# An attention stage on one core: the weighing of values done two key blocks at a time, value products and output projections moved to other slots

## The reference

```
c_q = h @ w_down_q.T ; c_kv = h @ w_down_kv.T              # latents, 128 wide
q, k, v = (c_q @ w_up_q.T), (c_kv @ w_up_k.T), (c_kv @ w_up_v.T)   # 16 heads of 64
q = _apply_rope_subspace(q, DR) ; k = _apply_rope_subspace(k, DR)
scores = jnp.einsum('bhqd,bhkd->bhqk', q, k) * scale
attn = jax.nn.softmax(scores, axis=-1)
out = jnp.einsum('bhqk,bhkd->bhqd', attn, v)
out = out.transpose(0, 2, 1, 3).reshape(b, s, H * DH)
out = out @ w_out.T + residual
```

## Time and profile before

| | |
|---|---|
| time, median of 3 runs | 2236.87 us (2235.29 to 2241.66) |
| the profiled execution's own time | 2242.25 us |
| its span, first to last instruction | 2240.6 us |
| mean granted TensorE clock | 0.940 |
| TensorE busy | 1922.1 us, 86% |
| VectorE, GpSimd busy | 1301.0 us, 1328.1 us |
| ScalarE busy | 895.0 us |
| instructions | 35323 |

### The profile page before, as it was taken

The page is one execution under the profiler, slowest core; times in us unless marked ns, Lnnn a source line. Parts: engine busy times, 40 slices in busy tenths (PEclk is TensorE's granted clock), DMA queues, the critical chain, the costliest instruction groups (busy, mean ns, idle before and its releaser), DMA issues. The chain is left out here.

```text
span 2240.6 us, 35323 instructions
## 1 busy us (share of the span) xinstructions
PE 1922.1 (86%) x12804; PEld 1333.1 (59%) x12804; DVE 1301.0 (58%) x1857; ACT 895.0 (40%) x1536; POOL 1328.1 (59%) x860
## 2 busy tenths in 40 slices
PE   5777649999999999999999964888885699998798
PEld 4666524454454545454454533666764699998798
DVE  6666436666656565666656523676663466565343
ACT  4554324433434343433434212333321355554454
POOL 2333228886868687887878632544544566666533
PEclk9888869999999999999999977999997899999899
DMA  3212231323222231323232213122213433323122
GB/s 102 75 56 75 86 106 40 76 48 95 57 67 69 50 93 34 95 48 95 57 85 58 57 29 126 32 70 77 61 57 105 133 81 81 77 51 107 29 45 42
DMA packets 81606, 158.63 MB, mean 71 GB/s; under 512 B 14496, under 2 KB 63520, under 8 KB 75552
## 3 DMA queue, kind: packets, MB, share of 16 engines
q1 hardware_dynamic: 66464, 133.40, 21.2%
q0 software_dynamic: 14592, 18.40, 5.0%
q10 hardware_dynamic: 432, 5.24, 0.6%
HBM read 80.84 MB, written 44.17 MB: 56 GB/s over the span
## 5 line engine op out<-in xcount | busy, mean ns | idle before, releaser
L916 ACT ACTIVATE a_pr<-a_pT 128x1024 f32<-128x1024 f32 x256 | 262.1, 1024 | 432.4 <-PE a_pT L739 432.4
L949 POOL TENSOR_TENSOR a_total<-a_total,a_pr 128x1024 f32<-128x1024 f32 x128 | 321.0, 2507 | 149.9 <-ACT a_pr L916 149.5
L821 DVE TENSOR_REDUCE a_row_max<-a_pG 128x2 f32<-128x1024 f32 x256 | 309.2, 1220 | 148.7 <-PE a_pG L713 148.6
L1832 DVE TENSOR_TENSOR c_h_lo<-c_h,c_h_hi 128x256 fp32r<-128x256 f32 x288 | 213.0, 757 | 195.0 <-ACT c_h_hi L1811 176.9
L752 PE MATMUL a_pA<-a_pr,a_v 128*64 128x512 f32 x1024 | 277.0, 619 | 0.1
L1811 ACT ACTIVATE c_h<-c_pU,c_b_c 128x256 f32<-128x256 f32 x288 | 138.8, 482 | 235.1 <-PE c_pU L103 234.5
L949 POOL TENSOR_TENSOR a_total<-a_pr 128x1024 f32<-128x1024 f32 x64 | 151.7, 2370 | 59.7 <-ACT a_pr L916 59.5
L930 POOL TENSOR_TENSOR a_by_cos<-a_by_cos,a_swapped 128x1024 f32<-128x1024 f32 x64 | 155.1, 2424 | 46.3 <-DMA a_swapped<-a_by_sin 46.2
L815 DVE TENSOR_TENSOR a_by_sin<-a_pG,a_sin 128x1024 f32<-128x1024 f32 x64 | 78.4, 1225 | 141.9 <-PE a_pG L103 136.9
L937 POOL TENSOR_TENSOR a_qk_lo<-a_by_cos,a_qk_hi 128x1024 fp32r<-128x1024 f32 x64 | 158.9, 2483 | 2.3 <-ACT a_qk_hi L886 2.3
L1868 POOL DMA_INDIRECT out_x<-c_y,c_ids x72 | 114.7, 1593 | 41.4 <-DVE c_y L1840 22.7
(11 more groups left out here) (248 smaller groups left out, 5072.7 us busy)
## 6 DMA issues: line engine op xcount, KB each, us to landing
a_swapped<-a_by_sin SPq DMA_DIRECT2D x256, 128.0 KB, 2.3
a_inv_by_head<-mid_inverses SPq DMA_DIRECT2D x32, 512.0 KB, 6.0
c_x_t<-mid_rows SPq DMA_DIRECT2D x37, 272.0 KB, 2.8
mid_latents<-f_c_parts SPq DMA_DIRECT2D x8, 1024.0 KB, 3.9
a_latent_parts<-mid_latents SPq DMA_DIRECT2D x8, 1024.0 KB, 7.2
d_raw<-in_weights SPq DMA_DIRECT2D x3, 2048.0 KB, 8.4
c_raw<-in_weights SPq DMA_DIRECT2D x3, 2048.0 KB, 8.1
f_x_t<-in_x SPq DMA_DIRECT2D x8, 512.0 KB, 3.9
```

The lines of the kernel that those rows point to most:

```text
L821: nc.vector.reduce_max(row_max[:, u % 2, :, t], pair[:], AX.X).then_inc(read, 1)
L916: nc.scalar.activation(pr[:, n % RP, :, :], pT[:], ACT.Exp, scale=SCALE).then_inc(exp_done, 1)
L949: nc.gpsimd.tensor_tensor(total[:, u % 2, :, :], before, pr[:, n % RP, :, :], ALU.add).then_inc(summed, 1)
L1832: nc.vector.tensor_tensor(h_lo[:, m % RH, :], h[:, m % RH, :], h_hi[:, m % RH, :], ALU.subtract).then_inc(h_lo_done[m % RH], 1)
```

## The change

In the order of TensorE's queue, `weigh` is called for two blocks of keys directly after each other: behind `shifted(u, 0)` the blocks 2 and 3 of the unit before, behind `shifted(u, 2)` the blocks 0 and 1 of the same unit. Behind `shifted` of slots 1 and 3 there is no weighing; in slot 1 `collect_sums` remains. Value products and output projections move from slots 1 and 2 to slots 1 and 3, in all queues at once. In slot 3 they stand behind `shifted` and ahead of `transpose_maxima`; on VectorE the addition stands ahead of `negate`, on ScalarE the copies ahead of the cast. After the last unit two weighings are left instead of one. Every instruction stays as it was; only the order changes.

```
@@ out_at and values_at
-            return (b - 1, 2 * (p - 3) + t - 1) if b >= 1 and p in (3, 4) and t in (1, 2) else None
+            return (b - 1, 2 * (p - 3) + t // 2) if b >= 1 and p in (3, 4) and t in (1, 3) else None
...
-            if p == 1 and t in (1, 2):
-                return b, 1, t - 1
-            if p == NP - 1 and t in (1, 2) and b + 1 < B:
-                return b + 1, 0, t - 1
+            if p == 1 and t in (1, 3):
+                return b, 1, t // 2
+            if p == NP - 1 and t in (1, 3) and b + 1 < B:
+                return b + 1, 0, t // 2
@@ TensorE's queue
                         shifted(u, t)
-                        if t >= 1:
-                            weigh(u, t - 1)
-                        elif u >= 1:
-                            weigh(u - 1, NT - 1)
+                        if t == 2:
+                            weigh(u, 0)
+                            weigh(u, 1)
+                        elif t == 0 and u >= 1:
+                            weigh(u - 1, 2)
+                            weigh(u - 1, 3)
...
-                weigh(UNITS - 1, NT - 1)
+                weigh(UNITS - 1, 2)
+                weigh(UNITS - 1, 3)
```

## The result

The changed kernel takes 2274.9 us (median of 4 runs, 2271.6 to 2280.7), the kernel before 2236.1 in the same comparison: ratio 1.018, 95% interval 1.016 to 1.020. The profiled execution of the changed kernel took 2276.02 us, 33.8 more than that of before.

The account below looks back on a forecast made before the run. TensorE's in-order queue, work and waits together, was taken as the bound. Unit terms sum to 5.98 us per batch element, 48 for eight, less 1 for the last unit: +47, 2284 us against the median 2236.87, range 2268 to 2303.

Parts of the forecast that it names:

- A second weighing costs 0.86, C alone 1.01: TensorE step prices in us: a weighing pair 1.87 instead of 1.01; C, collecting of sums, without a weighing 1.01.
- Plain unit +1.02: p = 0, 2, 5: +0.86 slot 0, -0.86 and +0.16 slot 1, +0.86 slot 2, nothing saved slot 3; +1.02 us.
- N: TensorE's transposing of the maxima, in slot 3; in plain units it waits for VectorE and cannot start before M2 + 3.04.
- M2: TensorE's scores for the row maximum, slot 2 (M0 to M3 for slots 0 to 3); VectorE takes the maximum.
- M1: Maximum scores of slot 1; needs the buffer Q filled, so waits for the second rotation product, ending at Q + 4.05.
- Unit with V +0.64: p = 1, 7, V being value products: +0.86 slot 0, 0 slot 1, -0.22 slots 2 and 3 together; sum +0.64 us.
- Q: TensorE's queries and keys matmuls, 1.59 us; the added weighing in slot 0 stands ahead of them.
- Unit with O +0.90: p = 3, 4, O being output projection (3.65 us): +0.86 - 0.22, and +0.26 from the later negation; sum +0.90 us.
- p = 5 and p = 6 +0.86: Both units together: latents load moves by only 0.86, its wait takes up 1.02, then -0.86 and +0.86; sum +0.86 us.
- first rival: The clock: new 1.45 us waits in plain units lower TensorE's clock, up to 36 us more, 2302 to 2320; chance 0.08.
- second rival: Faster: TensorE's own work decides, fewer tiling changes give -18 us, 2219; chance 0.05.
- third rival: No change: GpSimd sets the unit's length and TensorE's order doesn't matter, 2237 us; chance 0.04.

Follow-up runs that it names:

- experiment 3: Both orders with the maximum over 128 of 512 scores: changed order 2.8 us longer in attention; exponential also cut to 128 of 512 queries: 11.1 shorter.
- joined version: Kernel before with value products and output projections in slots 1 and 3, slot 2's maximum scores early, slot 0's weighing moved into slot 1: 2269.1 us, ratio 1.0115.
- experiments 1, 2 and 3: 1: kernel before with weighing pairs alone, 1.028, or products moved alone, 0.9966; 2: changed kernel, slot 2's maximum scores ahead of its pair, 1.0064; 3: see experiment 3.

## Why the prediction was right

The forecast was 2284 and +47, measured 2275 and +39 (33.6 in the traces). The mechanism came out as forecast: a weighing taken out of slots 1 and 3 lays bare waits for VectorE, and the second weighing in slots 0 and 2 is paid in full. The range of 2268 to 2303 held, but with 7 us to spare and a term that was off by 11. Term by term, in the element shown:

- *A second weighing costs 0.86, C alone 1.01.* Right: a pair 1.86, C with its wait 1.15.
- *Plain unit +1.02.* Right: p = 2 +1.03, by the three steps named (N held at M2 + 3.04, M1 held by the rotation product, two times 0.86 without cover). For p = 0 it was +0.65 (13.10 to 13.75): I took it as plain, but VectorE's reciprocal already made N wait longer in it.
- *Unit with V +0.64.* Right: p = 1 15.91 to 16.52, +0.61. V of slot 1 stands at the same distance from Q, 5.2.
- *Unit with O +0.90.* The 0.26 of the negation falls into the next unit: p = 3, 4 and 5 rose by 0.57, 0.80 and 1.27, together 2.64, forecast 0.90 + 0.90 + 1.02 = 2.82.
- *p = 5 and p = 6 +0.86.* The term that was mis-sized: 12.72 + 14.83 = 27.55 became 27.75, +0.20, of which 0.26 belong to O. Over all eight, p = 5 and 6 together changed by -2.5 us (from the first matmuls of the units), where 6.9 and 1.8 for O were forecast: 11 of the 13 us by which the sum was too large against the traces; p = 0 is most of the rest. What TensorE waited for in the 64 units before (in total, times, longest):

```profile
PE a_pG L720 <- DVE a_row_max L821: 15.6, 34, 0.7
PE a_pG L101 <- DMA a_latent_parts<-mid_latents: 10.4, 7, 2.6
PE a_pG L713 <- ACT a_qk_hi L886: 3.9, 4, 3.0
```

  and the first of these in the changed kernel:

```profile
PE a_pG L721 <- DVE a_row_max L825: 47.3, 34, 1.4
```

  The wait for latents fell to 0.4; the sum took 8.2 of it away. But it was the only wait that the sum knew in p = 6, and two things were left out. M0 waits there for the cast, the cast for GpSimd's rotation, and that for the swap: 3.9 us before, 3.0 of them in the last element, where no latents are loaded, and 0.9 in the changed kernel. And before, three units p = 6 (second, third and last element) ran at a granted clock of 0.89, 0.89 and 0.81; TensorE was busy for 13.95, 13.85 and 14.19 in them, against 12.74 in the element shown and 11.14 in the last element with the small spread. From these I estimate about 5 us, which the changed kernel, at 1.00 in all eight, didn't have. There is one trace of each, so how often the clock falls there is not known. The step that failed was that the swaps, and what waits behind them, move by 0.86 with Q. I tied the landing to the issue. SyncE's lines of the kernel before, and GpSimd's rotation:

```profile
776.75 1.12 SPq L656 DMA_DIRECT2D a_inv_by_head<-mid_inverses  x2
778.89 2.46 SPq L645 DMA_DIRECT2D a_swapped<-a_by_sin  x4
...
786.27 3.13 POOL L930 TENSOR_TENSOR a_by_cos<-a_by_cos,a_swapped 128x1024 f32<-128x1024 f32 x1 [1.70 <-DMA a_swapped<-a_by_sin]
```

  The same of the changed kernel:

```profile
795.47 1.12 SPq L657 DMA_DIRECT2D a_inv_by_head<-mid_inverses  x2
798.48 2.44 SPq L646 DMA_DIRECT2D a_swapped<-a_by_sin  x4
800.97 0.59 SPq L629 DMA_DIRECT2D a_latent_parts<-mid_latents  x1
```

  and what waits for the swaps:

```profile
805.04 2.37 POOL L934 TENSOR_TENSOR a_by_cos<-a_by_cos,a_swapped 128x1024 f32<-128x1024 f32 x1 [1.56 <-DMA a_swapped<-a_by_sin]
```

  Counted from the start of p = 5 (772.54 and 791.03), the swaps are issued 1.10 later than before, at 7.45, but the rotation starts only 0.28 later, at 14.01. By the profile a swap took up to 5.7 us from issue to landing before and up to 4.9 afterwards. The swaps stand behind a spread of 1 MB that is issued at a time fixed by the end of the unit before (4.2 and 4.4 us into p = 5). It doesn't move with Q. With the spread small, in the order before, the swaps are issued at 6.35 as before and the rotation starts at 11.99 instead of 13.73, without a wait. So it is shown that the spread holds up the swaps; how the queues share between the two was not looked at. With the spread small in both orders the change costs 45.9 in the attention stage, next to the 47 of the sum, but that is luck: p = 5 and 6 then rise by 14.3 over the eight elements where the sum has 6.9, since no wait is left that could take up the 1.02, and the other units rise by about 8 less than forecast.
- *The clock* (first rival) stayed at 1.00 behind 33 of the 34 waits of 1.4 in front of N. It fell once, behind such a wait in the third element; the pair of weighings there took 3.57 instead of 1.94:

```profile
589.23 3.57 PE L753 MATMUL a_pA<-a_pr,a_v 128*64 128x512 f32 x8
```

  That unit was 1.6 longer than its like, 18.14 against 16.52: the price that the rival had, once and not in each of 24 units.
- *TensorE's own work* decides (second rival): out as long as VectorE and ScalarE answer as they do. It is busy 14.7 less, where the rival said 18, but half of that is in p = 6. With the answers shortened the loss is gone (experiment 3); that a gain by the pairs would be left is not shown.
- *GpSimd sets the pace* (third rival) is wrong for this change: the unit's length did change. But the joined version runs into its chain.

Right behind N's wait stands that for the exponential of slot 3. The prediction had it, and rightly at nothing, since N's wait covered it. I forgot it in the expectations of experiments 1, 2 and 3, where N comes earlier, and it spoiled their sizes.

## What to carry to other kernels

In a queue that looks full, ask of each item what it covers. Moving it to save the cost of a switch (here 0.16, two single weighings of 1.01 against a pair of 1.86) can lay bare the wait that it stood in (here 1.0 a unit), and work that is moved to a busy slot is paid in full there. A wait has others behind it, so when one is removed, look for the next release before the gain is counted. And of a DMA that is issued later, ask what was in its way: it may land at nearly the same time.

## What the runs showed of the hardware

One instruction's time can spread widely where two engines work side by side. In the changed kernel VectorE's normalisation took 3.36 us in one unit and 1.22 in the next; GpSimd's addition beside the second took 3.44, against 2.37 for the one in the unit before. In both pairs the engine that started first took its usual time, and the other ended when about the sum of both had passed: 736.46 + 2.37 + 1.22 = 740.05, and it ended at 739.92; 750.31 + 1.22 + 2.37 = 753.90, and it ended at 753.76. It looks as if they took turns; no run here separates the two engines.

```profile
736.46 2.37 POOL L953 TENSOR_TENSOR a_total<-a_total,a_pr 128x1024 f32<-128x1024 f32 x1
...
736.56 3.36 DVE L846 TENSOR_TENSOR a_att<-a_att,a_inv_by_head 128x1024 f32<-128x1024 f32 x1
...
750.31 1.22 DVE L846 TENSOR_TENSOR a_att<-a_att,a_inv_by_head 128x1024 f32<-128x1024 f32 x1
750.32 3.44 POOL L953 TENSOR_TENSOR a_total<-a_total,a_pr 128x1024 f32<-128x1024 f32 x1
```
